# A third PSUM buffer for the edge products, key rows from DRAM, one softmax step an item, and sums two items later in a graph layer's edge loop

## The reference

```python
q = (x @ Wq + bq).reshape(n, H, C)          # n = 6250, H = 8 heads, C = 32
k, v = x @ Wk + bk, x @ Wv + bv             # alike
e = (edge_attr @ We).reshape(-1, H, C)      # edge_attr: 106250 x 256
alpha = einsum('ehc,ehc->eh', q[dst], k[src] + e) / sqrt(C)
ea = exp(alpha - segment_max(alpha, dst)[dst])
alpha = ea / (segment_sum(ea, dst)[dst] + 1e-16)
out = segment_sum((v[src] + e) * alpha[:, :, None], dst)
```

## Time and profile before

| | before |
|---|---|
| median of 3 runs | 2555.55 us (2554.52 to 2555.57) |
| the profiled execution | 2559.0 us, span of its instructions 2557.1 us |
| mean granted TensorE clock | 0.963 |
| busy: PE, DVE, ACT, POOL | 2374.8, 2032.8, 1578.5, 1809.4 us |
| share of the span that the edge loop takes | about two thirds |

### The profile page before, as it was taken

How to read it: one execution, slowest core, us unless ns; L and a number is a source line. 1 busy time by engine, 2 the same in 40 slices (tenths; PEclk the granted TensorE clock), 3 DMA queues, 4 the chain that set the end, 5 groups by cost and what they waited for, 6 DMA issues and landing times. The chain is left out here.

```text
span 2557.1 us, 61957 instructions
## 1 busy us (share of the span) xinstructions
PE 2374.8 (93%) x13310; PEld 1995.0 (78%) x13311; DVE 2032.8 (79%) x5261; ACT 1578.5 (62%) x4373; POOL 1809.4 (71%) x2136
## 2 busy tenths in 40 slices
PE   6998999999999999999999999999995647999998
PEld 3445888888888888888888888888883646999998
DVE  6865999999999999999999999999997773222222
ACT  1122676777777777777777767767774224666665
POOL 4223788888888888888888888878886104666666
PEclk9999999999999999999999999999998558999999
DMA  7326777777787777777777777777772753434443
GB/s 234 127 111 189 234 230 220 227 228 226 224 228 228 222 226 225 223 227 229 227 224 228 228 223 229 226 218 225 228 223 72 234 157 62 70 64 64 69 67 54
DMA packets 337663, 476.35 MB, mean 186 GB/s; under 512 B 61318, under 2 KB 268492, under 8 KB 337052
## 3 DMA queue, kind: packets, MB, share of 16 engines
q0 software_dynamic: 92576, 259.72, 38.4%
q1 hardware_dynamic: 238492, 213.23, 27.7%
q10 hardware_dynamic: 6288, 0.05, 0.1%
HBM read 425.40 MB, written 50.57 MB: 186 GB/s over the span
## 5 line engine op out<-in xcount | busy, mean ns | idle before, releaser
L809 POOL DMA_INDIRECT kv_ring<-vk_table,tab_c x880 | 860.6, 978 | 277.0 <-issue 179.6
L967 PE MATMUL ps_e<-we_sb,aT 128*128 128x256 f32 x3520 | 917.7, 383 | 25.3 <-DVE ve_ke L1055 21.4
L967 PEld LDWEIGHTS ps_e<-we_sb,aT 128*128 128x128 f32 x3520 | 601.1, 191 | 97.8 <-issue 46.0
L1050 DVE TENSOR_TENSOR ve_ke<-kv_ring,ps_e 128x512 f32<-128x512 f32 x880 | 600.5, 682 | 38.4 <-PE ps_e L971 22.0
L819 POOL TENSOR_TENSOR ve_ke<-ve_ke 128x256 f32<-128x256 f32 x880 | 551.3, 630 | 17.7 <-ACT factor L936 4.0
L1020 PE MATMUL ps_u<-ve_ke,sel 128*128 128x264 f32 x1760 | 546.1, 392 | 17.9 <-POOL ve_ke L819 7.6
L971 PE MATMUL ps_e<-q_slots,selT 128*128 x1760 | 517.7, 375 | 0.0
L896 ACT COPY aT<-ps_t 128x256 f32<-128x256 f32 x880 | 325.8, 370 | 301.0 <-PE ps_t L951 265.4
L1126 DVE SCALAR_TENSOR_TENSOR node_slots<-node_slots,same_tile,ps_u 128x264 f32 x880 | 423.4, 481 | 26.2 <-PE ps_u L1020 22.0
L971 PEld LDWEIGHTS ps_e<-q_slots,selT 128*128 128x128 f32 x1760 | 335.0, 190 | 45.8
L1038 DVE TENSOR_REDUCE alpha<-ve_ke 128x8 f32<-128x256 f32 x880 | 363.5, 413 | 1.9
(11 more groups left out here) (249 smaller groups left out, 2648.1 us busy)
## 6 DMA issues: line engine op xcount, KB each, us to landing
a_ring<-in_edge_attr SPq DMA_DIRECT2D x880, 128.0 KB
loc_c<-loc_table SPq DMA_DIRECT2D x220, 128.0 KB
kv_ring<-vk_table,tab_c POOLq DMA_INDIRECT x880
vk_table<-kv_out SPq DMA_DIRECT2D x49, 256.0 KB, 2.0
skip_table<-skip_out SPq DMA_DIRECT2D x49, 128.0 KB, 1.7
skip<-skip_table SPq DMA_DIRECT2D x7, 896.0 KB, 10.2
xn_table<-node_slots SPq DMA_DIRECT2D x7, 896.0 KB, 6.2
out<-node_slots SPq DMA_DIRECT2D x1, 6144.0 KB
```

The costliest lines, as they stand in the source:

```text
L809: g.indirect_dma_start(out=kv_ring[:, i % N_KV, :], out_offset=None, in_=vk_table, in_offset=bass.IndirectOffsetOnAxis(ap=tab_c[:, c % N_T ...
L967: t.matmul(ps_e[i % 2][:, 0:D], aT[i % 2][:, k * P:(k + 1) * P], we_sb[:, k, :], start=(k == 0), stop=(k == KD - 1))
L1050: v.tensor_tensor(ve_ke[:, to:ke + 1:ke - to, 0:D], kv.rearrange("p (t d) -> p t d", t=2), e[:, None, :].to_broadcast([P, 2, D]), ALU.add) ...
```

## The change

- `ps_e` has three buffers, taken in turn by the running number of the item; `project` waits for the item three before it. The softmax has one bank, `ps_s`; the turned result takes the place of the scores in it.
- The key rows of all chunks are made once in the first stage and written to two small tables in DRAM. In the loop SP loads them for each chunk by two broadcast transfers into `key_c`; the three key transposes of PE and ACT's copy of the last key are gone. The spread of the last minimum is an 8-column product.
- The steps `own` and `least` of DVE are cut in two, one instruction to an item.
- PE's steps move: scores from item 3 to 4, minima from 6 to 7, `turn_scores` from 10 to 13; ACT's exponential from 11 to 13. The lag of `sum` goes from 13 to 15, of `select` from 11 to 12; that of `add` (13) and `weigh` (15) stays.

```diff
-            ps_e = [ps3(f"ps_e{i}", [P, 512]) for i in range(2)]
+            ps_e = [ps3(f"ps_e{i}", [P, 512]) for i in range(N_E)]
...
-            ps_ak = ps3("ps_ak", [P, 512])
-            ps_rx = ps3("ps_rx", [P, 512])
...
+            ps_s = ps3("ps_s", [P, 512])
+            ps_a, ps_r, ps_d = ps_s[:, 0:P], ps_s[:, P:P + KW], ps_s[:, P + KW:P + KW + H]
+            ps_x = ps_a
...
             LAG = dict(weigh=FIRST_WEIGH + N_KV,
-                       select=FIRST_WEIGH,
-                       sum=FIRST_WEIGH + 2,
+                       select=FIRST_WEIGH + 1,
+                       sum=FIRST_WEIGH + 4,
                        add=FIRST_WEIGH + 2)
...
+            def load_keys(sp, c):
+                keys = key_c[c % 2]
+                sp.dma_start(keys[:, 0:P], first_table[c * CH:(c + 1) * CH, :].rearrange("(o i) h -> o (i h)", o=1).to_broadcast([P, P])
+                             ).then_inc(key_loaded[c % 2], 16)
+                sp.dma_start(keys[:, P:KW], last_table[c * CH:(c + 1) * CH + 1, :].rearrange("(o i) h -> o (i h)", o=1).to_broadcast([P, P + H])
+                             ).then_inc(key_loaded[c % 2], 16)
...
@@ SP, item 0 of a chunk, behind the loads of run_c and resets @@
+                            if c >= 2:
+                                sp.wait_ge(s["keys_apart"], at("keys_apart", c - 2))
+                            load_keys(sp, c)
@@ ACT @@
-                            act.wait_ge(s["keyed"], at("keyed", c - 1))
+                            act.wait_ge(key_loaded[1 - par], 32 * ((c - 1) // 2 + 1))
...
-                            nc.scalar.activation(not_f[:, :], ps_k, ACT.Abs, scale=-1.0, bias=run[:, 0:1])
+                            nc.scalar.activation(not_f[:, :], key_c[1 - par][:, :], ACT.Abs, scale=-1.0, bias=run[:, 0:1])
...
-                over_chunks(act, emit, what="select", parts={3: "apart", 4: "offs", 11: "exp"})
+                over_chunks(act, emit, what="select", parts={3: "apart", 4: "offs", 13: "exp"})
@@ PE, project @@
-                    pe.wait_ge(s["ve_added"], at("ve_added", c * CH + (i - 2)))
-                    pe.wait_ge(s["kq_ready"], at("kq_ready", c * CH + (i - 2)))
+                    pe.wait_ge(s["ve_added"], at("ve_added", c * CH + (i - N_E)))
+                    pe.wait_ge(s["kq_ready"], at("kq_ready", c * CH + (i - N_E)))
@@ PE, softmax steps @@
-                        elif kind == "keys":
...
                         elif kind == "scores":
                             pe.wait_ge(s["am_ready"], at("am_ready", c - 1))
-                            pe.wait_ge(s["keys_apart"], at("keys_apart", c - 1))
+                            pe.wait_ge(s["ea_ready"], at("ea_ready", c - 2))
...
                             pe.wait_ge(s["owned"], at("owned", c - 1))
+                            pe.wait_ge(s["shifted_ready"], at("shifted_ready", c - 1))
...
-                over_chunks(pe, emit, what="sum", parts={0: "keys", 3: "scores", 6: "minima", 10: "turn_scores"})
+                over_chunks(pe, emit, what="sum", parts={4: "scores", 7: "minima", 13: "turn_scores"})
@@ DVE @@
-                over_chunks(dve, emit, what="add", parts={3: "scan", 4: "scan_back", 6: "own", 7: "least", 8: "shift"})
+                over_chunks(dve, emit, what="add", parts={3: "scan", 4: "scan_back", 6: "own_first", 7: "own_last",
+                                                         8: "least_first", 9: "least_last", 10: "shift"})
@@ first stage, DVE @@
+                        for k, e in enumerate((0, P - 1)):
+                            v.tensor_tensor(keys_io[:, k, :, :], run_f[:, :, e:e + 1].to_broadcast([P, IB, H]),
+                                            head_row[:, None, :].to_broadcast([P, IB, H]), ALU.add).then_inc(keys_ready, 1)
```

More of the change, by code:

```diff
@@ L22 @@
 N_KV = 4
+N_E = 3
 N_A = 4
@@ L313, in _ @@
                     if j == LOCS_OUT:
+                        with nc.allow_non_contiguous_dma(reason="eight head keys of an item"):
+                            keys_to_tables()
                         sp.wait_ge(tables_ready, LOCS)
@@ L1041, in score @@
                 def score(c, par, i):
-                    e = ps_e[i % 2][:, 0:D]
+                    ps = ps_e[(c * CH + i) % N_E]
+                    e = ps[:, 0:D]
                     kv = kv_ring[:, i % N_KV, :]
@@ L1079, in softmax @@
                                                op1=ALU.min, accum_out=min_l[1 - par][:, :]).then_inc(s["owned"], 1)
-                    elif part == "least":
+                    elif part == "least_first":
                         dve.wait_ge(s["offs_ready"], at("offs_ready", c - 1))
```

64 lines of the change are left out of this document (36 added, 28 removed).

## The result

The changed kernel takes **2762.4 us** (median of 4 runs, 2760.1 to 2765.3) against 2555.0 us before: ratio 1.081, 95% interval 1.080 to 1.083. The profiled execution has a span of 2760.6 us, 203.5 more than that of before. The sign was right; the size, 207 us for the predicted 139, lies outside the range of 2622 to 2728.

What follows compares the result with a forecast made beforehand. PE and DVE, both near their ends, wait for each other; the new sum-add link and exponential stall lengthen the period 2.53 us to 33.70. 53 x 2.53 = 134, +139 with the ends: 2694 us median, range 2622 to 2728.

Steps and rivals of the forecast that it cites:

- Bound and period before: Edge loop before: PE 97.8% and DVE 96.3% busy, mostly waiting for each other; period 31.17 us a chunk.
- Part 1, key rows: Key rows loaded from DRAM by SyncE: taken at nothing, up to 0.3 us a chunk for the upper end.
- Part 2, one step an item: DVE's softmax steps one an item: waits between paired steps go, worth 0.3 us on DVE alone.
- Part 3, the ping-pong: DVE's add at item p waits for PE's sum at p+2: a link of 3.81 us for two items, 1.905 each.
- Part 4, the round trip: PE's projection 14 waits for ACT's copy behind the exponential: starts 2.35 us behind PE's product, stall 1.18 us every chunk.
- the list of what PE does ahead of the sum: Additions to PE's pace in the chain: 0.11 us at item 4, 0.32 at item 7, 0.51 at item 13.
- the same chain: Starts of add and sum followed item by item through a chunk until they repeat: period 33.70 us, 2.53 more than before.
- The upper bound of 0.20 for the load: PE's load of 16 registers at item 13: issue gap of 0.20 us, giving period 33.90 and 2705 us.
- the first period: Pass 1 of the edge loop: has the stall of part 4, taken at +1 us.
- 1.05 us for the rescale: DVE's rescale step in the chain, once a chunk: 1.05 us, read as 1026.73 - 1025.68 in the kernel before.
- something else feeds the loop late: Rival: GpSimd waits for the exponential ahead of item 15's gather, or SyncE is late; above 2728 us, 7 in 100.

Runs made afterwards that it cites:

- The repaired versions: Changed kernel with sums one item later, scores turned at item 12, SyncE's tables later, gather ahead of first weighing: 2556.7 us; with rescaling inside item 13 too: 2546.3 us.
- experiment 6: Kernel before with key rows from DRAM and one softmax bank: 2563.8 us; also three buffers, with sums, select, PE's softmax steps and exponential one item later: 2560.0 us.
- the version with all feeds in time: Changed kernel with sums one item later, scores turned at item 12, SyncE's tables at item 3, item 15's gather ahead of the first weighing: 2556.7 us.
- experiment 2: Changed kernel with DVE's adds one item earlier (lag 12), three items ahead of the sum they wait for: 4530 us.
- experiment 1: Changed kernel with the sums one item later instead of two (sum lag 14): 2600.8 us.
- experiment 3: Changed kernel with adds two items later: 2656.0 us; with ACT's exponential at item 14 instead: 2724.3 us; with both (third run, first timeline): 2682.0 us.
- Experiment 7: Changed kernel with PE's load of node numbers just ahead of projection 14: 2739.0 us; with GpSimd's mask ahead of item 5's gather too: 2711.9 us.
- experiment 8: DVE's two rescaling steps moved between reduction and multiplication of item 13: repaired version (2556.7 us without the edit) 2546.3 us, kernel before 2550.8 us.

## Why the prediction was right in sign and too small

- **Bound and period before** (DVE and PE near their ends, waiting for each other): right. The repaired versions all end where DVE's work ends.
- **Part 1, key rows**: taken at nothing; with the bank 0.3% by experiment 6, nothing in the period. Right within the bound.
- **Part 2, one step an item**: taken at -0.3 us a chunk. No run shows this term by itself; the version with all feeds in time gains nothing over the kernel before. What it moved was mis-sized: it put PE's turn three items later and the exponential two, which I priced on PE alone.
- **Part 3, the ping-pong**: right in mechanism and size; the waits are fewer and longer than said, because DVE's steps fill the link at most of the items 3 to 10. The link was 3.81 to 3.83 us where one item carries it (experiment 2), and removing it by one item took 162 us (experiment 1).
- **Part 4, the round trip**: right in size, 2.33 for 2.35 us, one in each chunk. There is luck in it: ACT starts 0.87 us behind PE's product (0.79 taken), and PE starts 0.06 behind ACT's copy (1013.21 for 1012.80 + 0.35; 0.15 taken). A stall that is taken away is not all gained: 38 us of 66. The wait for SyncE's edges that appeared instead (experiment 3) is the likely reason; no run has both mended.
- **The step that failed is the list of what PE does ahead of the sum.** At item 4 it had 0.11 us, the transpose alone, and not that its input comes from GpSimd, behind a gather that in turn waits for DVE: +0.33 us a chunk. At item 13 it had nothing for the load of 16 node numbers, "behind a busy PE this shows nowhere", although the same chain says that PE is no longer busy: 0.39 us in one chunk's rows, 0.47 in the period. Experiment 7 takes away 50 us; 53 x (0.47 + 0.33) = 42 of them are these two, the rest lies in the longer chunks or is not placed. The upper bound of 0.20 for the load was a misread row: the 0.20 in brackets counts only from the modelled end of the product before. From start to start the same row shows 249.42 - 248.64 = 0.78 us, where the pair without a load between takes 247.74 - 247.31 = 0.43. The load cost 0.35 us there already:

```profile
247.31 0.59 PE L971 MATMUL ps_e<-q_slots,selT 128*128 x2
247.74 0.38 PE L951 MATMUL ps_t<-ident,a_ring 128*128 128x128 f32 x2
...
248.64 0.59 PE L971 MATMUL ps_e<-q_slots,selT 128*128 x2
```

- **The whole 68 us.** Most chunks of the changed kernel take 34.45 us instead of 33.70: 53 x 0.75 = 40 us, the two terms above. The chain stands for such an undisturbed chunk, but I held it against a mean of before that includes longer ones (31.17; most take 30.7). The changed kernel has longer chunks too, and they are 17 us that the chain has not. Some 4 us are the first period, 39.5 us: its first add waits 4.80 us since nothing is in flight yet, and I took 1 us. Another 4 us come from the mean of 400 to 1800 us, 31.17, where the whole loop has 31.09, and 3 us from the profiled execution, which here does not lie above the median. This is worked out from the distances of the rescales, not tested.
- **Two errors that cancelled**: I took 1.05 us for the rescale; in the changed kernel it takes 0.81 (1017.20 to 1018.01), because no weighing runs beside it (last section). And I had nothing for DVE's loads of node numbers, which leave a gap of 0.28 us ahead of the product behind item 12 (81 such gaps, 18.4 us, between 400 and 1800 us).
- **The range**: the rival "something else feeds the loop late" had 7 in 100. It was right that GpSimd and SyncE were made late, wrong that their gathers and edges would show: the waits that showed were a mask and a register load. Three small unknowns of 0.3 us in 53 chunks are 48 us. The upper end should have carried them.

## What to carry to other kernels

When two engines hand work back and forth, put the whole circle together, add its hand-overs, and divide by the number of items that it spans; compare this with the slowest engine's own time for an item. Below it the distance costs nothing, above it all, so one item of lag is worth 162 us here and the next one 1770. One more buffer adds one item to the span: here it paid for consumers one item later, not for two. Every step whose result travels through other engines stays as early as it can. Once an engine stalls, its register loads and every instruction queued ahead of a late one come into the sum, on each queue that was moved.

## What the runs showed of the hardware

- Hand-overs between PE and DVE are short and constant: four successive circles, each with two of them, agree to 0.02 us (experiment 2). An indirect gather on GpSimd starts later. In the changed kernel DVE's product ends at 1018.41 + 0.68 = 1019.09, and the gather that waits for it starts 0.79 later, where PE and DVE take 0.15:

```profile
1018.41 0.68 DVE L1075 TENSOR_TENSOR ve_ke<-kv_ring,ps_e 128x512 f32<-128x512 f32 x1
...
1019.88 0.97 POOL L843 DMA_INDIRECT kv_ring<-vk_table,tab_c  x1 [0.77 <-DVE ve_ke L1075]
```

It is the gather, not GpSimd as a whole: in the first timeline of experiment 3 the weighing starts at 1011.49, 0.18 behind ACT's factor:

```profile
1011.05 0.26 ACT L970 ACTIVATE factor<-ps_s,carried 128x8 f32<-128x8 f32 x1
```

- An indirect gather and a weighing need 1.79 us of GpSimd an item although they count as 1.61 us of busy time: 0.16 us of issue ahead of every gather is not in the busy share.
- A product of two SBUF tiles on DVE takes 0.42 to 0.88 us for the same 128 x 256 elements (rescale row: 415/659/884 ns), and of the pair of rescaling steps now one, now the other is long, 0.73 + 0.15 and 0.42 + 0.57. GpSimd's weighing ran beside the long one each time, from 1024.90 in the version without and from 1020.56 in the one with the edit of experiment 8, where it is itself stretched:

```profile
1024.90 0.62 POOL L853 TENSOR_TENSOR ve_ke<-ve_ke 128x256 f32<-128x256 f32 x1
```

```profile
1020.56 0.75 POOL L853 TENSOR_TENSOR ve_ke<-ve_ke 128x256 f32<-128x256 f32 x1
```

The Trainium skill (SBUF — State Buffer, SBUF: two separate sides) says that a DVE operation with two SBUF inputs and a GpSimd operation that reads SBUF exclude each other for a whole instruction. The trace agrees that they delay each other: the long step ends 0.29 us (1025.81 for 1025.52) and 0.02 us (1021.33 for 1021.31) behind the weighing, which is less than the 0.42 and 0.15 that the steps take alone. The changed kernel is the counter-test: between 400 and 1900 us its first rescaling step overlaps with a weighing in 1 of 43 chunks, and all 43 take 0.42 to 0.49 us. In the kernel before 42 of 49 take 0.64 us or more, and every one of the 42 overlaps with a weighing.
- PE's load of 16 register values costs 0.4 us when PE has caught up with its queue, and 0 when it stands in a wait (experiment 7).
